# A decoder layer on one core: another order of work where the slot attention hands over to the cross attention, and in the first slot steps

## What is computed

```python
x = x + _L0_attn_ref(_layernorm(x), ...)      # gated slot attention, 4 heads, 64 slots
x = x + _L0_xattn_ref(_layernorm(x), ctx, ctx, side, side, mask, attn_mask, ...)   # 16 heads of 8
x = x + _L0_ffn_ref(_layernorm(x), ...)       # 8 LoRA experts, top 2
# cross attention:
scores = jnp.einsum('bhtd,bhsd->bhts', q, k) * scale + attn_mask
scores = jnp.where(pad, -inf, scores) + spatial_bias + directional_bias
out = jnp.einsum('bhts,bhsd->bhtd', softmax(scores), v)
```

## Time and profile before

| | |
|---|---|
| median of 3 runs | 604.25 us (603.99 to 606.11) |
| the profiled execution | 605.81 us |
| its span, first to last instruction | 604.1 us |
| TensorE matmul busy | 542.7 us (90%) |
| VectorE, ScalarE, GpSimd busy | 482.7, 398.6, 355.7 us |
| mean granted TensorE clock | 0.962 |
| slot stage about | 4 to 225 us |
| cross stage about | 204 to 450 us |
| median load of 512 KB of biases, issue to landing | 7.2 us |

### The profile page before, as it was taken

The page is one execution under the profiler, slowest core; times in us unless marked ns, Lnnn a source line. Parts: engine busy times, 40 slices in busy tenths (PEclk is TensorE's granted clock), DMA queues, the critical chain, the costliest instruction groups (busy, mean ns, idle before and its releaser), DMA issues.

```text
span 604.1 us, 17291 instructions
## 1 busy us (share of the span) xinstructions
PE 542.7 (90%) x5328; PEld 416.1 (69%) x5328; DVE 482.7 (80%) x1945; ACT 398.6 (66%) x1033; POOL 355.7 (59%) x362
## 2 busy tenths in 40 slices
PE   4689999999998559999999999999978999999986
PEld 3457777777776436777777777777766778788864
DVE  2478887887886358999999999999988688888872
ACT  2668878878775238889999999999965333333221
POOL 6234555456544657888888888888933233334430
PEclk9799999999998868999999999999987899999999
DMA  6910000000000075898989888888700000000000
GB/s 169 239 21 2 1 1 1 0 0 0 2 0 2 7 126 101 153 168 152 159 155 156 155 155 149 148 151 162 128 3 1 2 17 19 17 17 19 17 19 17
DMA packets 84429, 42.47 MB, mean 70 GB/s; under 512 B 4378, under 2 KB 84132, under 8 KB 84388
## 3 DMA queue, kind: packets, MB, share of 16 engines
q1 hardware_dynamic: 83234, 41.63, 37.5%
q10 hardware_dynamic: 1154, 0.33, 0.2%
HBM read 39.86 MB, written 2.10 MB: 69 GB/s over the span
## 4 chain that ended last, share of the span: by engine, by line
PE 50%; DVE 17%; issue 16%; ACT 7%; POOL 7%; DVEq 0%; ACTq 0%; POOLq 0%
PE banks L873 6%; PE banks L907 6%; PE banks L920 5%; PE banks L453 5%; ACT c_P L954 4%; PE banks L1228 4%; DVE c_P L1026 3%; DVE shared L714 3%; PE banks L1252 3%; PE banks L896 3%; PE banks L417 2%; PE banks L444 2%; PE banks L499 2%; PE banks L886 2%; DVE banks L687 2%
## 5 line engine op out<-in xcount | busy, mean ns | idle before, releaser
L1121 POOL TENSOR_TENSOR c_bias<-c_fside,c_cm 128x2048 f32<-128x2048 f32 x32 | 146.2, 4568 | 27.5 <-PE banks L873 16.9
L954 ACT ACTIVATE c_P<-c_P,c_min 128x128 f32<-128x128 f32 x512 | 156.7, 391 | 2.9 <-DVE c_min L1026 2.9
L1026 DVE CUSTOM_DVE_ANT_0 c_P<-banks,c_bias 128x128 f32<-128x128 f32 x512 | 116.4, 284 | 5.6 <-issue 3.0
L907 PEld LDWEIGHTS banks<-ident,c_P 128*128 128x128 f32 x512 | 59.3, 144 | 30.0 <-issue 23.2
L907 PE MATMUL banks<-ident,c_P 128*128 128x128 f32 x512 | 76.0, 282 | 3.7 <-DVE shared L1062 3.7
L1062 DVE COPY shared<-banks 128x512 f32<-128x512 f32 x96 | 65.7, 685 | 0.0
L1228 PE MATMUL banks<-um,lb_s 128*128 128x512 f32 x192 | 56.1, 407 | 2.7 <-ACT shared L1285 1.9
L1464 POOL TENSOR_TENSOR xs<-shared,xs 128x512 fp32r<-128x512 f32 x8 | 10.7, 1337 | 69.9 <-ACT xs L1295 69.9
L1285 ACT ACTIVATE shared<-banks,bi_col 128x512 f32<-128x512 f32 x32 | 22.0, 687 | 39.2 <-PE banks L1228 39.2
L1228 PEld LDWEIGHTS banks<-um,lb_s 128*128 128x128 f32 x192 | 34.6, 190 | 19.1 <-ACT shared L1285 12.5
L794 POOL TENSOR_TENSOR shared<-shared 128x512 f32<-128x512 f32 x16 | 20.4, 1275 | 38.1 <-ACT shared L585 38.1
(11 more groups left out here) (195 smaller groups left out, 1310.6 us busy)
## 6 DMA issues: line engine op xcount, KB each, us to landing
c_fside<-in_fside_Bx16xSxS_dram SPq DMA_DIRECT2D x64, 512.0 KB, 7.2
c_ctx<-in_ctx_dram SPq DMA_DIRECT2D x32, 64.0 KB, 5.2
out_dram<-shared SPq DMA_DIRECT2D x8, 256.0 KB, 2.3
X<-in_x_dram SPq DMA_DIRECT2D x3, 512.0 KB, 5.4
kmask_sb<-in_mask_BxS_bf_dram SPq DMA_DIRECT2D x1, 512.0 KB, 6.8
X<-in_x_dram SPq DMA_DIRECT2D x2, 128.0 KB, 3.0
c_P<-in_L_ffn_wi_dram SPq DMA_DIRECT2D x1, 256.0 KB
c_P<-in_L_ffn_lora_B_dram SPq DMA_DIRECT2D x1, 256.0 KB
```

The source lines that it names most:

```text
L907: last = nc.tensor.transpose(bank(2 + i % 2)[:, 128 * j:128 * j + 128], P[:, q, XG * i + j, :], ident[:])
L954: last = nc.scalar.activation(P[:, par, h, :], P[:, par, h, :], ACT.Exp, bias=mn[:, par, h:h + 1], scale=-1.0)
L1026: last = nc.vector.tensor_tensor_reduce(out=P[:, o, h, :], in0=bank(SCORE_BANKS[i])[:, 128 * j:128 * j + 128], in1=fm[:, o, h, :], scale=- ...
L1121: nc.gpsimd.tensor_tensor(fm[:, q, :, :], fs[:, q, :, :], bc(cm[:], XH), ALU.add).then_inc(C["fm"], 1)
```

## The change

Every engine function takes a list of names, `only`, so that a step can be issued in pieces. With it:

- *First slot steps.* ScalarE does pair 0's gate functions before it normalises pair 1, and pair 1's before pair 2. TensorE transposes pairs 1 and 2 earlier, before the cumulative sum of the step, and pair 2's projections before pair 0's slot logits. VectorE does the sigmoid product before statistics and attention in steps 1 and 2.
- *Passage.* The cross stage's steps -3 to 2 are dealt in pieces between those of the slot stage's steps 16 to 19, on all four compute engines. Statistics of batch 0 come before slot step 16 on VectorE. On GpSimd slot step 17 is cut in three: the outputs and pair 15's weights come after the score biases of batch 0 and before those of batch 1, the squares after them.
- *Banks.* Batches 0 to 2 use banks (1, 4, 5, 1); the fourth score waits until VectorE has read the first.
- *Masks.* A step's mask tile, for batch n+2 at the start of step n, is now that of batch n+3 at the end of step n.
- *Loop.* The cross loop runs n = 4 to 27 instead of 2 to 25.

```diff
+        FIRST_BANKS = (1, 4, 5, 1)
+        FIRST = 3
+        def score_banks(batch):
+            return FIRST_BANKS if isinstance(batch, int) and batch < FIRST else SCORE_BANKS
...
+                places = score_banks(n + 1)
                 for i in range(NI):
                     rows = slice(32 * i, 32 * i + 32)
+                    if places[i] in places[:i]:
+                        need(pe, C["tt"], 4 * n + 5 + places.index(places[i]))
...
             def masks():
-                need(dve, C["fm"], n + 2)
-                km = kmask_sb[:, bass.ds((n + 2) * T, T)]
+                need(dve, C["fm"], n + 3)
+                km = kmask_sb[:, bass.ds((n + 3) * T, T)]
...
-            with engine.Fori(1, B // 2 - 3, 2) as m:
+            with engine.Fori(2, B // 2 - 3, 2) as m:
```

GpSimd's queue:

```diff
             x_peeled(cross, -3)
-            gsa_peeled(gsa, PAIRS + 1)
+            gsa_peeled(gsa, PAIRS)
...
             x_peeled(cross, -2)
+            gsa_peeled(gsa, PAIRS + 1, "outputs")
+            gsa_peeled(gsa, PAIRS + 1, "weights")
+            x_peeled(cross, -1)
+            gsa_peeled(gsa, PAIRS + 1, "squares")
+            x_peeled(cross, 0)
             gsa_peeled(gsa, PAIRS + 2)
-            x_peeled(cross, -1)
+            x_peeled(cross, 1)
             gsa_peeled(gsa, PAIRS + 3)
```

ScalarE's:

```diff
             gsa_normalise(act, 0)
-            for t in range(0, 2):
-                gsa_peeled(gsa, t)
+            gsa_peeled(gsa, 0, "inputs", "gates")
+            gsa_normalise(act, 1)
+            gsa_peeled(gsa, 1, "inputs", "sigmoids", "decays", "gates")
+            gsa_normalise(act, 2)
+            gsa_peeled(gsa, 1, "slots")
...
-            x_peeled(cross, -3)
-            gsa_peeled(gsa, PAIRS + 1)
+            gsa_peeled(gsa, PAIRS + 1, "turned", "roots")
             x_peeled(cross, -2)
-            gsa_peeled(gsa, PAIRS + 2)
+            gsa_peeled(gsa, PAIRS + 1, "exps", "outputs")
             x_peeled(cross, -1)
+            x_peeled(cross, 0, "exps1", "exps2", "inputs", "exps3")
+            gsa_peeled(gsa, PAIRS + 2, "turned")
+            x_peeled(cross, 0, "exps0", "keys", "queries", "turned3")
+            gsa_peeled(gsa, PAIRS + 2, "roots")
+            x_peeled(cross, 1, "exps1")
+            gsa_peeled(gsa, PAIRS + 2, "outputs")
+            x_peeled(cross, 1, "exps2", "inputs", "exps3", "exps0", "sums", "keys", "queries", "turned3")
             gsa_peeled(gsa, PAIRS + 3)
```

VectorE's:

```diff
-            gsa(1, 1, False, True, False, False, False, True)
+            gsa(1, 1, False, True, False, False, False, False, ("silu",))
+            gsa(1, 1, False, True, False, False, False, True, ("statistics", "slots", "values"))
...
-            gsa_peeled(gsa, 2)
+            gsa_peeled(gsa, 2, "silu")
+            gsa_peeled(gsa, 2, "statistics", "attention", "logits", "slots", "sums", "values", "gates")
...
-            x_peeled(cross, -3)
-            gsa_peeled(gsa, PAIRS + 1)
+            x_peeled(cross, -3, "statistics", "aggregates")
+            gsa_peeled(gsa, PAIRS)
             dve.wait_ge(s_km, 16)
-            x_peeled(cross, -2)
-            gsa_peeled(gsa, PAIRS + 2)
-            x_peeled(cross, -1)
+            x_peeled(cross, -3, "normalise", "masks")
+            gsa_peeled(gsa, PAIRS + 1, "attention")
+            x_peeled(cross, -2, "statistics", "aggregates")
+            gsa_peeled(gsa, PAIRS + 1, "logits")
+            x_peeled(cross, -2, "normalise", "masks")
+            gsa_peeled(gsa, PAIRS + 1, "mix", "sums")
+            x_peeled(cross, -1, "scores0", "scores1", "scores2", "scores3")
+            gsa_peeled(gsa, PAIRS + 1, "stream")
+            x_peeled(cross, -1, "statistics", "aggregates", "values", "normalise", "masks")
+            x_peeled(cross, 0)
+            gsa_peeled(gsa, PAIRS + 2, "mix")
+            x_peeled(cross, 1, "statistics", "scores0")
+            gsa_peeled(gsa, PAIRS + 2, "stream")
+            x_peeled(cross, 1, "turned0", "scores1", "turned1", "scores2", "aggregates", "scores3", "outputs", "turned2", "stream",
+                     "values", "normalise", "masks")
+            x_peeled(cross, 2)
             gsa_peeled(gsa, PAIRS + 3)
```

TensorE's:

```diff
-            gsa_peeled(gsa, 1)
+            gsa_peeled(gsa, 1, "inputs")
+            gsa_peeled(gsa, 1, "decays", "gates", "values", "slots")
...
-            gsa_peeled(gsa, 2)
+            gsa_peeled(gsa, 2, "inputs", "attention")
+            gsa_peeled(gsa, 2, "decays", "gates")
+            gsa_peeled(gsa, 2, "logits", "values", "slots")
...
-            x_peeled(cross, -3)
-            gsa_peeled(gsa, PAIRS + 1)
+            gsa_peeled(gsa, PAIRS + 1, "attention", "turned", "squares")
             pe.wait_ge(G["silu"], PAIRS)
             x_peeled(cross, -2)
-            gsa_peeled(gsa, PAIRS + 2)
-            pe.wait_ge(G["lgts"], PAIRS)
+            gsa_peeled(gsa, PAIRS + 1, "logits", "mix")
+            pe.wait_ge(G["shift"], PAIRS)
+            x_peeled(cross, -1, "scores")
+            gsa_peeled(gsa, PAIRS + 1, "outputs", "project")
+            x_peeled(cross, -1, "inputs", "queries", "values")
+            x_peeled(cross, 0, "scores")
+            pe.wait_ge(G["rt"], PAIRS - 2)
+            x_peeled(cross, 0, "turned0", "inputs")
+            pe.wait_ge(G["x1"], PAIRS - 2)
+            x_peeled(cross, 0, "turned1", "queries")
+            gsa_peeled(gsa, PAIRS + 2, "turned")
+            x_peeled(cross, 0, "turned2", "turned3", "values")
+            pe.wait_ge(C["ptD"], 3)
+            gsa_peeled(gsa, PAIRS + 2, "squares", "mix")
+            x_peeled(cross, 1, "scores")
+            pe.wait_ge(C["ptA"], 1)
+            gsa_peeled(gsa, PAIRS + 2, "outputs", "project")
...
+            gsa_peeled(gsa, PAIRS + 3, "squares")
             pe.wait_ge(G["un"], PAIRS)
-            x_peeled(cross, -1)
-            gsa_peeled(gsa, PAIRS + 3)
+            x_peeled(cross, 2, "scores")
...
+            gsa_peeled(gsa, PAIRS + 3, "project")
```

More of the change, by code:

```diff
@@ L43, in hold, with named @@
     engine.sem_inc(passed, 1)
+def named(only):
+    return lambda flag, name: flag and (only is None or name in only)
 def upto(count, most):
@@ L389, in inner, with gsa_tensor @@
             return ap[:, :, None].broadcast_to([128, ap.shape[1], n])
-        def gsa_tensor(pe, t, par, gate, turn, intra, mix, finish, ahead):
+        def gsa_tensor(pe, t, par, gate, turn, intra, mix, finish, ahead, only=None):
             def x_turned():
@@ L500, in project_out @@
                 last.then_inc(G["y"], 1)
-            if intra:
+            on = named(only)
+            if on(intra, "attention"):
                 attention()
-            if mix:
+            if on(mix, "turned"):
                 weights_turned()
-            if finish:
+            if on(finish, "squares"):
                 square_sums()
-            if turn:
+            if on(turn, "decays"):
                 decay_sums()
-            if intra:
+            if on(intra, "logits"):
                 slot_logits()
-            if gate:
+            if on(gate, "inputs"):
                 x_turned()
-            if mix:
+            if on(mix, "mix"):
                 slot_mix()
-            if gate:
+            if on(gate, "gates"):
                 queries_keys_gates()
-            if turn:
+            if on(turn, "values"):
                 values()
-            if mix:
+            if on(mix, "outputs"):
                 outputs()
-            if turn:
+            if on(turn, "slots"):
                 s_turned()
-            if finish:
+            if on(finish, "project"):
                 project_out()
@@ L534, in gsa_normalise, with gsa_scalar @@
             last.then_inc(G["xn"], 1)
-        def gsa_scalar(act, t, par, gate, turn, intra, mix, finish, ahead):
+        def gsa_scalar(act, t, par, gate, turn, intra, mix, finish, ahead, only=None):
             def x_turned():
@@ L646, in gsa_stats, with gsa_vector @@
                 nc.vector.bn_aggr(meanvar[:, b, :], stats[:, b, :]).then_inc(G["aggr"], 1)
-        def gsa_vector(dve, t, par, gate, turn, intra, mix, finish, ahead):
+        def gsa_vector(dve, t, par, gate, turn, intra, mix, finish, ahead, only=None):
             def log_sigmoid():
@@ L730, in statistics @@
                 gsa_stats(dve, t + 1)
-            if intra:
+            on = named(only)
+            if on(intra, "attention"):
                 causal_attention()
-            if ahead:
+            if on(ahead, "statistics"):
                 statistics()
-            if turn:
+            if on(turn, "silu"):
                 silu()
-            if intra:
+            if on(intra, "logits"):
                 slot_logits()
+            if on(intra, "logits"):
                 slot_maxima()
-            if turn:
+            if on(turn, "slots"):
                 slots()
-            if mix:
+            if on(mix, "mix"):
                 causal_mix()
-            if intra:
+            if on(intra, "sums"):
                 slot_sums()
-            if turn:
```

(29 more changed lines are left out.)

241 lines of the change are left out of this document (121 added, 120 removed).

## The result

The changed kernel takes 671.99 us (median of 4 runs, 664.51 to 676.5); the kernel before 605.18 (603.99 to 608.08). By these medians it is 67 us slower. The ratio, 1.101 with an interval of 1.091 to 1.111, is smaller because it leaves out the two longest runs (674.76 and 676.5, over 1.5% above the shortest) as slow ones; by it the change costs 61 us. Some 4 us faster was forecast, and both figures lie far outside the range. The profiled execution took 669.22, its span is 667.2, 63.1 more than before's 604.1.

A forecast was written before the change was run, and what follows sets the result against it. GpSimd's queue order, through head-of-line waiting, was taken to bound the passage, with TensorE's clock lowered. Span 604.1 - 1.6 - 2.35 + 0.3 = 600.45, 602.1 in all, 600.5 against the 604.25 median; range 595.5 to 605.0 us.

The forecast's parts named there:

- the one about the loop: Cross loop: its cyclic order is left as it was, so nothing is added for it.
- My slower rival: Cross steps -1, 0 and 1: lone fourth scores at the lower clock keep TensorE's gaps; 606.9 us, chance 0.1.
- if the cross steps change their period: Cross loop: a sign that the prediction is wrong; the old period was expected from batch 5 on.
- First slot steps: Start of slot stage: gate functions ahead of the next pair's normalising gain 0.8 to 2.5 us, taken as 1.6.
- Passage: Slot to cross stage, up to batch 4's biases: gain 6.25 us at the upper clock, 2.35 in the walk taken.
- My low clock stretches: Passage: TensorE's clock low near 207 to 210 and 214 to 220.6 us only, giving gain 2.35.
- rival 2: Passage: one more low clock stretch makes its gain 0, leaving the first steps' 0.8 us; 603.5 us, chance 0.2.
- The lone fourth scores: Passage, batches 0 to 2: three times a wait for bank 1 plus 1.1 to 2.05 us of TensorE.
- GpSimd's early weights: Passage: pair 15's weights delay biases 1 by 3.8 us, covered by late key 1; no gain by itself.
- Rival 4: Passage: GpSimd's early weights are the bound, adding 1 to 2 us; 602 us, chance 0.45 shared with the forecast.
- The steps behind biases 4: Two steps after batch 4's biases: pair 15's remaining projection and addition take back 0.3 us.
- Expert stage unchanged: Expert stage: nothing is changed there, so its old length was expected and nothing added.

The follow-up runs named there:

- placed: after_pad11 again with more runs (12), the changed kernel with VectorE's cross loop starting at 578; 605.27 us, ratio to before 0.9984.
- first_only: Kernel before with the new first slot steps, old passage, four score banks and 12 empty steps (loop start 578); 605.65 us, ratio 0.9991.
- after_pad11: Changed kernel with 11 empty semaphore steps on VectorE ahead of its cross loop (start 578 instead of 567); 603.24 us, ratio to before 0.9979.
- after_pad128: Changed kernel with 128 empty steps on VectorE ahead of its cross loop (start 695); 673.41 us.
- bank6_b1: placed with batch 1's fourth score in bank 6 instead of a second turn of bank 1; 598.35 us, ratio to before 0.9867.
- weights_late: placed with pair 15's weights on GpSimd moved back behind batch 1's score biases, keys and root; 605.08 us, ratio to before 0.9983.
- after_short: Changed kernel with VectorE's cross loop of two batches a turn instead of four (142 instructions, same start); 606.24 us, ratio to before 1.0013.
- before_pad117: Kernel before with 117 empty steps on VectorE ahead of its cross loop, which then starts at 567; 659.88 us, ratio 1.0901.

## Why the prediction was wrong, and where it was right

**The step that failed** is the one about the loop: "The diff leaves the cross loop's cyclic order as it was ... I add nothing for either." The first half held: between returns the steps run at the old period. But I costed the loop only by what its instructions do and in what order, not by where in the queue they lie. Moving 117 instructions from behind the loop to ahead of it put its start at 567, and there the loop touches a fourth piece and is fetched anew each turn: each of five returns costs VectorE some 11 us (7.1 + 4.9 at 322 to 335 us), 55.6 in all, 66 with what follows. My slower rival had the wrong mechanism (the lone scores) and a price of 2.65; no rival had the loop. The text did name "if the cross steps change their period" as what would make it wrong. The profile before held a warning but no price: its instruction queues moved no packet from 280 to 400 us, four returns included, so the loop lived off what was kept, and I didn't ask whether it would still be kept.

The rest was tested by the placed kernels, with the loop's cost out of the way. There 3.65 us of gain were forecast and 1.0 was measured.

- *First slot steps, 1.6 us, right in mechanism, gone by the end.* In the changed kernel's timeline ScalarE's first Abs is at 12.39 (said: near 12.5), the cumulative sum at 16.91 (17.1), the first slot logits on VectorE at 31.51, better than my range of 32 to 33.7 and 2.96 ahead of the earlier trace rows (in placed and first_only, where the granted clock from 15 to 30 us is 0.89 instead of 1.00, they start at 33.20 and 33.22):

```profile
12.39 1.02 ACT L552 ACTIVATE shared<-banks 128x1024 f32<-128x1024 f32 x1 [3.87 <-PE banks L413]
...
16.91 1.13 PE L422 MATMUL banks<-shared,tri_centred 128*128 128x512 f32 x2
...
31.51 0.70 DVE L696 TENSOR_TENSOR banks<-banks,shared 128x512 f32<-128x512 f32 x1 [1.97 <-PE banks L458]
```

  It didn't last: the lower clock came later instead of not at all, and I take that for the reason, though no run sets it apart. In the kernel before the low stretch was at 20 to 26; in the changed kernel the windows show

```profile
15.00:30.00 15.00, 11.72 (x64) 8.20 (x62) 10.27 (x24) 10.63 (x19) 4.55 (x15) 1.00 1.18 248
30.00:45.00 15.00, 11.41 (x72) 8.78 (x71) 9.19 (x17) 8.12 (x14) 5.40 (x9) 0.77 0.22 36
```

  The lead of 3.0 us at pair 0's weights (34.40, before 37.43) is 1.5 at pair 3's in this execution; there it is 1.9 in after_pad11, 1.7 in after_pad128, 1.3 in bank6_b1, 0.3 in weights_late, and none in after_short, placed and first_only (69.86, 69.89 and 69.81, before 69.72). I had let the clock decide how large the lead is up to the slot logits, and not what it does behind them. That is the first term of the sum that was mis-sized: 1.6 said, 0 to 1.9 measured, and nothing in the medians of first_only.
- *Passage, 2.35 us, right in shape, too large.* Counted from pair 15's weights to biases 4 it gave 2.2 us in after_pad11, 1.6 in the changed kernel and 1.3 in placed. Biases 4 started at 238.45 in after_pad11, inside the 238 to 239 named, and at 241.45 in placed. My low clock stretches were too few: the windows from 205 to 220 in after_pad11 have a granted clock of 0.50 throughout,

```profile
205.00:220.00 15.00, 12.57 (x55) 8.15 (x48) 7.13 (x46) 6.42 (x21) 10.11 (x6) 0.50 0.45 82
```

  where I had held the scores and projections of 210.6 to 214 at the upper level. So the truth lay between my forecast and rival 2, the gain "hidden anyway".
- *The lone fourth scores, right.* They appear three times, behind waits of 2.77, 1.12 and 1.30 us, and take 1.12 to 2.07. The rule of the Trainium skill, page TensorEngine Tiling (Array Packing), section Gotcha 1: PSUM Pressure, which I weighed in the prediction, agrees: the score on a used bank ran by itself. Batch 1's cost 3.2 us with its wait, and taking it away shortened the passage by 3.1 to 4.0 us, the whole of it on the path. Only batch 1's was taken away; that all three together are the largest cost of the new passage, and why its gain is small, is argued from the rows.
- *GpSimd's early weights, the edit of the title, costed rightly.* Said: 3.8 us of the start of biases 1, covered by the late key 1, nothing of it in the time. Measured: 3.4 us, and no difference in time. Rival 4, that the early weights bound the passage, is refuted by the same run.
- *The steps behind biases 4, 0.3 us taken back.* Measured in placed: from biases 4 to the end 362.65 us against 361.75, so 0.9 comes back; 0.5 of it lies between batches 4 and 6 (14.80 against 14.31), where pair 15's remainder is, and 0.5 between batches 16 and 31. With that, the 0.9 that placed leads at biases 4 is gone in its profile, and the 1.0 us of the medians is all that remains.
- *Expert stage unchanged*: from biases 31 to the end 167.79 against 167.75.
- *A wrong reading.* Rival 2 gives the old cross steps as 7.8 us; from biases 4 to 31 of the kernel before they take 7.2 (194.00 over 27). No sum used it.

**What stays open.** Every run fits a loop that is kept as long as it touches three pieces of 128 instructions and is fetched anew when it touches a fourth. With a border at 578, 25 starts in 128 are bad for 282 instructions, 553 to 577. But only one bad remainder (55) and two good ones (13, 66) were tried, so the width of the bad stretch is argued, not shown. Nor is it shown why the second wait is up to 4.9 us in the changed kernel and 2.1 in before_pad117 at the same start, 14 us in all.

## What to carry to other kernels

Before moving instructions across a hardware loop, count each engine's queue: on VectorE a loop of more than two pieces of 128 instructions can be fast or some 8% slower by its place alone (51.5 us of 605), and a handful of empty steps ahead of it, or half as much unrolling (1.9 us here), is the cure. Of the other engines no run here tests it: TensorE's loop of 298 instructions moved from start 733 to 870 with the change, and from 230 to 510 us its waits hold no issue wait. The mark in a profile is "issue" idle time at a loop's first instruction, as many times as the loop returns, with more packets on the instruction queue. And when steps are interleaved, first look for the bank or buffer that frees a matmul of its wait: one bank more was worth over 3 us of a passage in which the whole reordering had won 1.3 to 2.2.

## What the runs showed of the hardware

- A loop of 282 instructions on VectorE ran its returns without stalls at starts 450, 525 and 578 (issue waits at the loop's first instruction of up to 0.3 us), and at 567 and 695 with 7.1 to 7.7 us at the return and 2.1 to 4.9 us a few instructions on. A loop of 386 stalled at 450, up to 8.0 us; one of 142 at 567 did not (up to 0.4 us).
- The fetches are 8 KB pieces (0.37 MB in 46 packets), five in each turn of the stalling loop, and a piece begins at VectorE's instruction 578 and at 706. The Trainium skill's page Runtime: NRT & Kernel Launch, section Instruction fetch mechanics, says that a taken branch whose target isn't in the current window forces a fetch before execution goes on. The trace agrees, with 7.1 us beside it. The page also says that a refill is 16 KiB; here the measurement differs, the pieces on this queue are 8 KB. From 280 to 400 us the kernel before went round its loop of 282 instructions with no fetch at all.
- A stall of 12 us on one engine at each return also takes the TensorE clock to its lower level: the window from 330 to 345 us is granted 0.50 all through, and the loss is 66 us where VectorE's own waits are 55.6.
- The same kernel (placed, after_pad11) had medians of 605.27 and 603.24 us on two occasions and profiled spans of 604.1 and 598.9. Of the 5.2 between the spans, 2.1 lie ahead of pair 3's weights, 0.9 between there and biases 4, and 2.2 behind biases 31, where the granted clock from 440 to 460 us is 0.74 in the one and 0.91 in the other, and from 460 to 480 us 0.91 and 1.00. What is gained in a stretch that borders on the lower level is therefore to be judged on medians of paired runs, not on one profile.
